# Gated cross-attention with a routed expert layer on one core: the first attention batch in a new order on four engines and the DMA queue, the first slot's rows in two halves, and a third one-hot ahead of the last selection

## What is computed

```
def _layernorm(x): m = mean(x); v = var(x); return (x - m) / sqrt(v + 1e-5)

# x: (2, 512, 1024), ctx: (2, 1024, 1024)
q1 = clip(round(layernorm(x) / s1 + z1), 0, 255);  a = (q1 - z1) * s1
q2 = clip(round(ctx / s2 + z2), 0, 255);           c = (q2 - z2) * s2
x  = x + tanh(g_xattn) * matmul(a, c)

y = layernorm(x)
logits = y @ W_gate + b_gate                       # 8 experts
top 2 experts per row
x = x + tanh(g_ffn) * mean over the 2 of relu(y @ W_e[e] + b_e[e])
```

## Time and profile before

| | |
|---|---|
| median of 3 runs | 359.78 us (358.92 to 360.76) |
| the profiled execution | 359.12 us, its span 357.4 us |
| mean granted TensorE clock | 0.964 |
| PE busy | 323.5 us, 91% of the span, 1695 instructions |
| PE weight loads busy | 251.0 us, 70% |
| DVE busy | 226.3 us, 63% |
| ACT busy | 139.9 us, 39% |
| POOL busy | 113.0 us, 32% |
| HBM | 62.43 MB read, 18.87 MB written |

### The profile page before, as it was taken

The page is one execution under the profiler, slowest core; times in us unless marked ns, Lnnn a source line. Parts: engine busy times, 40 slices in busy tenths (PEclk is TensorE's granted clock), DMA queues, the critical chain, the costliest instruction groups (busy, mean ns, idle before and its releaser), DMA issues.

```text
span 357.4 us, 6929 instructions
## 1 busy us (share of the span) xinstructions
PE 323.5 (91%) x1695; PEld 251.0 (70%) x1704; DVE 226.3 (63%) x345; ACT 139.9 (39%) x124; POOL 113.0 (32%) x135
## 2 busy tenths in 40 slices
PE   0598899999599999999999999999999999999960
PEld 0134366589547888888888888888888888888840
DVE  2898999977889653799668326832349334934220
ACT  3774878789103701656172017201154015401100
POOL 3553464000024023415335335123332333233310
PEclk9999999998579999999999999999999999999995
DMA  6999568475327986799989955975439953455233
GB/s 224 413 409 385 220 253 347 166 261 230 159 85 300 410 285 135 192 383 318 417 251 326 358 125 131 395 237 117 88 103 358 330 109 86 100 116 118 29 88 59
DMA packets 23004, 81.46 MB, mean 228 GB/s; under 512 B 3152, under 2 KB 3152, under 8 KB 22992
## 3 DMA queue, kind: packets, MB, share of 16 engines
q1 hardware_dynamic: 16656, 58.76, 42.9%
q0 software_dynamic: 6192, 22.55, 26.6%
q10 hardware_dynamic: 144, 0.01, 0.0%
HBM read 62.43 MB, written 18.87 MB: 228 GB/s over the span
## 4 chain that ended last, share of the span: by engine, by line
PE 80%; DVE 12%; issue 2%; DMA 2%; POOL 1%; ACT 0%; POOLq 0%; DVEq 0%; ACTq 0%
PE ps L1262 61%; PE ps_y L1238 5%; PE ps L1065 4%; DVE st L744 4%; PE ps_q L1124 2%; PE ps_s L1124 2%; PE ps L1042 2%; PE ps_y L1097 2%; DMA par<-in_small_dram 2%; DVE xt L808 1%; PE ps L1150 1%; PE ps L1072 1%; DVE u8c L790 1%; DVE lnv L760 1%; DVE mv L746 1%
## 5 line engine op out<-in xcount | busy, mean ns | idle before, releaser
L1262 PE MATMUL ps<-w_hi,yT_hi 128*128 x320 | 126.5, 395 | 0.5 <-DVE yT_lo L994 0.5
L1262 PE MATMUL ps<-w_hi,yT_lo 128*128 x320 | 124.8, 390 | 0.0
L1262 PE MATMUL ps<-w_lo,yT_hi 128*128 x320 | 124.5, 389 | 0.0
L880 DVE TENSOR_TENSOR w_lo<-stage,w_hi 128x2048 f32 (+1 forms) x32 | 72.0, 2287 | 13.2 <-ACT w_hi L679 11.8
L679 ACT ACTIVATE w_hi<-stage 128x2048 f32 x28 | 52.5, 1912 | 59.1 <-PE ps L1262 47.2
L504 POOL DMA_INDIRECT out_dram<-res,sidx x20 | 32.5, 1627 | 133.7 <-DVE res L1028 121.1
L1025 DVE TENSOR_TENSOR res<-ps,bias 128x512 f32<-128x512 f32 x40 | 27.6, 689 | 65.5 <-issue 34.1
L1262 PEld LDWEIGHTS ps<-w_hi,yT_hi 128*128 128x128 f32 x320 | 60.1, 188 | 12.7 <-issue 0.9
L1262 PEld LDWEIGHTS ps<-w_hi,yT_lo 128*128 128x128 f32 x320 | 60.1, 188 | 12.8
L1262 PEld LDWEIGHTS ps<-w_lo,yT_hi 128*128 128x128 f32 x320 | 60.2, 188 | 11.8
L666 ACT ACTIVATE yT_hi<-ps_y 128x1024 fp32r<-128x1024 f32 x21 | 21.4, 1020 | 114.5 <-PE ps_y L1238 114.5
(11 more groups left out here) (163 smaller groups left out, 264.7 us busy)
## 6 DMA issues: line engine op xcount, KB each, us to landing
stage<-in_L_ffn_W_e_dram SPq DMA_DIRECT2D x32, 1024.0 KB, 7.3
stage<-in_ctx_dram SPq DMA_DIRECT2D x16, 512.0 KB, 11.6
xt<-in_x_dram SPq DMA_DIRECT2D x8, 512.0 KB, 11.4
y_scratch<-y SPq DMA_DIRECT2D x8, 512.0 KB, 3.9
out_dram<-xt SPq DMA_DIRECT2D x8, 512.0 KB, 3.0
bias<-in_L_ffn_b_e_dram SPq DMA_DIRECT2D x8, 512.0 KB, 4.2
y_rows<-y_scratch,gidx POOLq DMA_INDIRECT x22
out_dram<-res,sidx POOLq DMA_INDIRECT x20, 6.4
```

The costliest lines, as they stand in the source:

```text
L880: dve.tensor_tensor(w_lo[:, dst], stage[:, CK * c:CK * (c + 1), :].rearrange("p k h -> p (k h)"), w_hi[:, dst].bitcast(f32), ALU.subtract) ...
L1262: last = pe.matmul(ps[q][:, h * 512:(h + 1) * 512], lhs[q][:, k, :], w[:, bass.ds(woff + k * D + h * 512, 512)], start=(k == 0 and lhs is ...
```

## The change

- **x and ctx loads (SP).** x tile 3 is loaded after ctx tile 7, the second batch's ctx tiles come ahead of x tiles 6 and 7, and all four chunks of the first expert's weights are issued before the first stores.
- **ACT.** `quantise_ctx(0)` is put ahead of the first `std`, tiles 1 and 2 follow it, and the order is new down to `keep_yT(2)`.
- **POOL.** It centres ctx tile 4 in place of 7 (DVE does the reverse) and x tiles 4, 5 and 7, which DVE did.
- **DVE.** `split_d` and ctx tiles 6 and 7 come before the statistics of x tile 3; the statistics of x tiles 4 to 7 come later.
- **PE.** `transpose_q1(2)` goes behind the first two folds; the column sums of the second batch are made in one piece, and the transposes of y move between the halves of `attend`.
- **One-hots (DVE).** Three, not two, before the selection of the last three tiles.
- **First slot.** Its eight transposes signal after four; ACT and DVE evacuate the two halves of four; the second weight chunk's low part is made in two pieces, one ahead of the halves and one behind; PE starts its products after the first half. `keep_clock(10)` becomes `keep_clock(6)`.

The diff's core:

```
-        POOL_CEN = (0, 1, 2, 3, 5, 7, 8, 9, 10, 11, 12, 13, 14, 15)
-        DVE_CEN = (4, 6)
+        POOL_CEN = (0, 1, 2, 3, 4, 5, 8, 9, 10, 11, 12, 13, 14, 15)
+        DVE_CEN = (6, 7)
-        POOL_Q1, DVE_Q1 = (0, 1, 2, 6), (3, 4, 5, 7)
+        POOL_Q1, DVE_Q1 = (0, 1, 2, 4, 5, 6, 7), (3,)
...
@@ POOL
             centre_ctx(0)
             centre_ctx(1)
+            centre_ctx(2)
             centre_q1(0)
-            centre_ctx(2)
             centre_q1(1)
...
@@ ACT
             std(1, 2, 2, 2)
             split_hi0(0)
+            keep_q1T(6)
+            normalise(2)
             keep_yT(2)
-            keep_q1T(6)
...
@@ DVE
             derive()
+            split_d()
+            quantise_ctx(6)
+            quantise_ctx(7)
+            centre_ctx(6)
+            centre_ctx(7)
             x_stats(3)
             scales(0, 2, 2, 2)
+            keep_colsum_lo(0)
             quantise_x(3)
             centre_q1(3)
-            centre_ctx(4)
-            quantise_ctx(6)
-            centre_ctx(6)
-            quantise_ctx(7)
-            split_d()
+            x_new(0)
...
             make_onehot(1)
+            make_onehot(2)
             select(1)
...
-            split_lo(1, 2, slice(CW, 2 * CW))
+            split_lo_row(CK)
             dve.wait_ge(s_eh, 1)
-            evacuate_lo(0)
+            evacuate_lo(0, slice(0, KT // 2)).then_inc(s_el, 1)
+            dve.wait_ge(s_eh, 2)
+            evacuate_lo(0, slice(KT // 2, KT)).then_inc(s_el, 1)
+            split_lo_row(CK + 1).then_inc(s_lo, 1)
...
@@ PE
             fold(0)
             fold(1)
+            transpose_q1(2)
             transpose_q1(3)
...
-            transpose_y(0)
-            column_sums(KT + 4, KT + 6)
+            column_sums(KT + 4, 2 * KT)
             pe.wait_ge(s_rs, 1)
             transpose_q1(5)
-            transpose_y(1)
-            column_sums(KT + 6, 2 * KT)
             attend_after(4)
             attend_half(4, 0)
-            gate(0)
+            transpose_y(0)
             attend_half(4, 1)
             fold(4)
-            transpose_y(2)
+            transpose_y(1)
+            gate(0)
             attend_after(5)
             attend_half(5, 0)
             gate(1)
             transpose_q1(6)
             attend_half(5, 1)
             fold(5)
-            transpose_y(3)
+            transpose_y(2)
             attend_after(6)
             attend_half(6, 0)
+            transpose_y(3)
...
-            transpose_slot(0)
-            keep_clock(10)
+            for k in range(KT):
+                last = pe.transpose(ps_y[:, k, :], y_rows[0][:, k * P:(k + 1) * P], ident_f[:, :])
+                if k == KT // 2 - 1:
+                    last.then_inc(s_t0, 1)
+            last.then_inc(s_tp, 1)
+            keep_clock(6)
```

More of the change, by code:

```diff
@@ L322, in _ @@
                 load_x(i)
-            for k in (0, 1):
+            for k in (0, 1, 2):
                 load_ctx(k)
             load_x(2)
-            load_ctx(2)
-            load_x(3)
             for k in range(3, KT):
                 load_ctx(k)
-            for j in range(TPB):
-                load_x(TPB + j)
-                load_ctx(KT + j)
+            load_x(3)
+            load_ctx(KT)
+            load_ctx(KT + 1)
+            load_x(4)
+            load_ctx(KT + 2)
+            load_x(5)
+            load_ctx(KT + 3)
+            load_ctx(KT + 4)
             sp.dma_start(wg[:, :, :], W_gate.rearrange("(k p) e -> p k e", p=P)).then_inc(s_wg, 16)
-            for k in range(KT + TPB, 2 * KT):
+            for k in range(KT + 5, 2 * KT):
                 load_ctx(k)
-            load_w0(0)
-            load_w0(1)
+            load_x(6)
+            load_x(7)
+            for c in range(NCH):
+                load_w0(c)
             store_y(0)
             store_y(1)
-            load_w0(2)
-            load_w0(3)
             store_x_new(0)
@@ L441, in _ @@
             centre_ctx(1)
+            centre_ctx(2)
             centre_q1(0)
-            centre_ctx(2)
             centre_q1(1)
             centre_ctx(3)
+            centre_ctx(4)
             centre_ctx(5)
-            centre_ctx(7)
             centre_ctx(8)
+            centre_ctx(9)
+            centre_ctx(10)
             centre_q1(2)
-            for k in range(KT + 1, 2 * KT):
+            for k in range(KT + 3, 2 * KT):
                 centre_ctx(k)
+            centre_q1(4)
+            centre_q1(5)
             pool.wait_ge(s_att, TPB)
@@ L596, in _ @@
             act.activation(lnv[:, 0, T1, 0:1], eps[:, :], ACT.Sqrt)
+            act.wait_ge(s_inv, 1)
+            quantise_ctx(0)
             std(0, 0, 2, 1)
-            quantise_ctx(0)
             quantise_ctx(1)
+            quantise_ctx(2)
             quantise_x(0)
-            quantise_ctx(2)
             quantise_x(1)
-            std(0, 2, 2, 2)
[L604 to L608, removed]
+            quantise_ctx(3)
+            quantise_ctx(4)
+            keep_q1T(0)
+            quantise_ctx(5)
+            keep_q1T(1)
+            quantise_ctx(8)
+            keep_colsum_hi(0)
+            std(0, 2, 2, 2)
+            quantise_ctx(9)
+            quantise_ctx(10)
             quantise_x(2)
-            quantise_ctx(8)
+            quantise_ctx(11)
             keep_q1T(2)
[L612 to L617, removed]
             keep_q1T(3)
             quantise_ctx(12)
-            quantise_x(5)
[L621 to L626, removed]
+            quantise_ctx(13)
+            quantise_ctx(14)
+            std(0, 4, 2, 3)
+            quantise_ctx(15)
+            quantise_x(4)
+            quantise_x(5)
             keep_q1T(4)
             keep_q1T(5)
-            std(1, 2, 2, 2)
+            std(1, 0, 2, 1)
+            keep_colsum_hi(1)
+            normalise(1)
+            keep_yT(0)
+            sum_q1(4)
+            std(0, 6, 2, 4)
             keep_yT(1)
[L631 to L634, removed]
             quantise_x(6)
             quantise_x(7)
+            std(1, 2, 2, 2)
             split_hi0(0)
+            keep_q1T(6)
+            normalise(2)
             keep_yT(2)
-            keep_q1T(6)
             std(1, 4, 1, 3)
@@ L685, in step @@
                 act.wait_ge(s_tp, slot + 2)
-                evacuate_hi(slot + 1, 1 - q)
+                evacuate_hi(1 - q, slice(0, KT)).then_inc(s_eh, 2)
                 with act.If(nxt > 0):
@@ L948, in _ @@
             slot_matrix(1)
-            for i in range(2, NT):
+            for i in range(3, NT):
                 make_onehot(i)
@@ L1252, in step @@
                 pe.wait_ge(s_free, slot * HB + 1)
-                pe.wait_ge(s_el, slot + 1)
+                pe.wait_ge(s_el, slot * 2 + 1)
                 for h in range(HB):
@@ L1256, in step @@
                         if h == 0 and k == CK:
+                            pe.wait_ge(s_el, slot * 2 + 2)
                             pe.wait_ge(s_g[1 - q], turn * 16 + (16 if q == 0 else 32))
```

59 lines of the change are left out of this document (30 added, 29 removed).

## The result

| | before | changed |
|---|---|---|
| median, same chip | 359.57 us (358.92 to 360.76, 4 runs) | 364.21 us (364.08 to 365.30, 4 runs) |
| profiled execution | 359.12 us, span 357.4 | 365.30 us, span 363.6 |
| mean granted TensorE clock | 0.964 | 0.954 |

The account below looks back on a forecast made before the run. PE was taken to bound the kernel, mostly waiting for DVE, with hardly a gap from 43.60 to 71.33. Terms -0.9 + 4.05 - 0.4 - 0.45 = +2.3 on the median of 359.78 gave 362.1 us; 8-in-10 range 358.7 to 364.3.

Parts of the forecast that it names:

- step 3: Second batch: three new PE waits, for y of tile 0, q1 of tile 6 and y of tile 2; +4.05 us.
- the second wait: Second batch: PE waits for q1 of x tile 6 from POOL, 9.8 against 9.25 of PE work; 0.56 us.
- step 1: First scales on DVE: held by POOL's centring of ctx tiles 0 to 2, ready at 14.05 instead of 12.66.
- the fifth is held: First scales: DVE's fifth instruction waits for POOL's centring of tile 1; if not, scales are ready at 13.05.
- step 2: First batch, up to the sums of q1 at 43.60: a gain, -0.9 us, bounds -2.4 to 0.
- bound of 0 for the latest rise: First batch: no gain if PE's clock rises only at 24.3 and all of POOL's holds on DVE apply.
- the forecast rise at 22.7: First batch: PE's clock goes from 1.2 to 2.4 GHz at 22.7, 5.1 after its last gap.
- between the two bounds: First batch: as the number of slow matmuls varies by run, anything from -2.4 to 0 us may come.
- Steps 4 to 6: Moved loads cost 0; third one-hot gives -0.4 us; first slot in halves gives -0.45 us.
- The faster one: Rival, chance 0.14: clock falls behind the last gates, saving 2.2; with early front and low bounds -2.4 us, 357.4.
- Much slower: Rival, chance 0.18: no first-batch gain, a longer second batch, one-hot and slot gains kept; +4.1 us, 363.9.
- the late rise and the fourth hold: Clock rises late, so the first batch gains 0; one more hold adds 0.9 us to the second batch's waits.

Follow-up runs that it names:

- The three runs with products added in front: Changed kernel plus twelve dummy products (363.63); new first batch, mended with nine, under old second batch (365.82); changed kernel plus both ACT moves and twenty (360.25).
- the square root first: Changed kernel with one ACT call moved: std(1, 0) goes ahead of keep_q1T(5); 364.14 us, ratio 1.0111 to the kernel before.
- the slot alone: Kernel before with only the first slot's part of the change (halves, weight chunk in two pieces, keep_clock(6)); 360.05 us, ratio 0.9987.
- more added work: Changed kernel with two ACT calls moved (std(1, 0) earlier, split_hi0(0) later) and twenty dummy PE products; 360.25 us, ratio 0.9983 to the kernel before.
- the two runs with added products: Kernel before with the first slot in halves, third one-hot, and 6 or 12 dummy products around the last gates; 359.02 and 359.01 us.
- one or both ACT edits: Changed kernel with std(1, 0) ahead of keep_q1T(5) (364.14), split_hi0(0) behind normalise(2) (363.53), or both moves (365.18 us).
- the trace shown above: Kernel before with the first slot in two halves and the third one-hot, none of the first batch's changes; 360.19 us, ratio 0.997.

## Why the prediction was off by half

- **Right: the sign of the whole, and the second batch.** All three waits of step 3 are there, with the engines named: 1.46 (forecast 1.6), 0.43 (0.56), 1.76 (1.85), 3.65 against 4.0; the stretch grew by 3.4 against 4.05. (The terms listed for the second wait add up to 9.9, not 9.8, which would make it 0.7.)
- **Right: step 1.** Timeline of DVE in the changed kernel:

```profile
10.88 0.65 DVE L772 SCALAR_TENSOR_TENSOR lnv<-mv,eps,lnv 128x2 f32<-128x2 f32 x1
...
11.96 0.90 DVE L776 TENSOR_SCALAR lnv<-lnv,drv 128x2 f32<-128x2 f32 x1
...
13.10 0.94 DVE L778 TENSOR_SCALAR lnv<-lnv,par 128x2 f32<-128x2 f32 x1
```

  and of POOL:

```profile
10.49 1.05 POOL L428 TENSOR_SCALAR q<-u8c 128x1024 bf16<-128x1024 uint8 x1 [6.58 <-ACT u8c L534]
11.80 2.22 POOL L428 TENSOR_SCALAR q<-u8c 128x1024 bf16<-128x1024 uint8 x2 [0.26 <-ACT u8c L534]
```

  The second, fifth and seventh instruction end with POOL's three centrings, and the scales end at 14.04 (forecast 14.05). The choice that the fifth is held was right. The Trainium skill (SBUF — State Buffer, Who interferes with whom) gave the same answer, and the trace agrees.
- **Wrong: step 2, -0.9 forecast, +2.3 measured.** The walk held to the correction (fold at 31.16, forecast 31). Then two terms failed. DVE's quantising and centring of x tile 3 were priced at 0.8 and some 0.6, with one hold of 1.06; both were held by POOL's centrings at 31.12 and 32.25:

```profile
31.05 1.67 DVE L788 TENSOR_SCALAR u8x<-xt,lnv 128x1024 uint8<-128x1024 f32 x1
32.75 1.41 DVE L796 TENSOR_SCALAR q<-u8x 128x1024 bf16<-128x1024 uint8 x1
```

  so that the two took 3.1, not 2.5, and with 0.3 from ahead of them (DVE's half ended at 31.02, not 30.7) PE attended tile 2 at 35.53, not 34.5: 1.0. And the forecast took each product there at 0.23, when the gaps it had itself put ahead of them (for the correction, for q1 of tile 3, for the slab) took the clock down: 5.84 - 3.63 = 2.2. The three runs with products added in front, where these ran at full speed, show that this was the gaps' doing. The forecast used the clock only for when it rises, never for whether it falls again. Its bound of 0 for the latest rise lay 2.3 below what came, and below all four other traces of the same front (+0.8 to +1.4).
- **The Trainium skill's rule on the clock.** The prediction quoted the Trainium skill (TensorE: Matmul & The Clock Gate, Part 1): activity releases the throttle, and the number of slow matmuls isn't to be fitted. The traces agree with the second: the first eight products of the attention, in eight traces with the same instructions up to there, take

```profile
19.68 3.51 PE L1084 MATMUL ps<-q,q1T 128*128 128x512 bf16 x8
```

```profile
19.62 2.16 PE L1084 MATMUL ps<-q,q1T 128*128 128x512 bf16 x8
```

  in the changed kernel and with the square root first, and between these two in the others. (The slow pace is read from the products; the granted clock of the profile reads 1.00 here.) So the forecast rise at 22.7, which came at about 23.0 in the profiled execution, was luck: it was taken from the one rise in the kernel before. And "between the two bounds" was wrong, since the range had no second fall in it.
- **Steps 4 to 6.** The moved loads cost nothing on PE's path. Gates and one-hots gave -0.3 for -0.4: five one-hots take 3.07, as costed, while the gates are 0.4 slower. At the last weight chunk PE was 8.39 behind the transposes (forecast 8.25; before 8.81, which the forecast read as 8.7), and at the slot's end -0.3 is left, for -0.45. The first product came 3.28 behind them, not 2.2, though DVE's first half was there after some 2.0 (its two halves take 1.29 from 112.15 on); what PE waited for isn't settled (with the square root first, the slot alone and more added work it came after 2.53 to 2.75), and the weight chunk behind it makes it worth nothing.
- **Rivals.** The faster one needed the clock to fall behind the last gates. It fell in front of them, as before; the two runs with added products show that 2.4 of gate time lay there, as its 2.2 had it. "Much slower" (363.9) is nearest to the 364.2 measured, yet by another mechanism than the late rise and the fourth hold it was made of. The range ended at 364.3 because of that rival, so that it held 364.2 is luck too.
- **What failed, in one line.** Step 2: the front was forecast to win 0.9 and lost 2.3 in the profiled execution (0.8 to 1.4 in four others). The term at fault is the clock, put at "rises once" (2.2 in this trace), and beside it the holds of DVE's two instructions and a start that was late by 0.3 (1.0 together).

## What to carry to other kernels

When a change opens a gap on PE, price it as a range, from the gap alone to the gap plus the work behind it at the lower clock, and look at the granted clock of that stretch before you believe a sum of waits. When a repair takes a wait away and the time stays, look for the next wait and for slow products behind it, and at more than one trace where the clock is at play. A few products of no use in a gap that can't be closed were cheap here (twenty of them, with two moves on ACT, took 4 us back). And an order written by hand hangs together over its stages: the new front under the old middle was 1.4% slower than the kernel before, and no faster than the changed one.

## What the runs showed of the chip

Behind gaps of about 1 us the granted clock fell to 0.50, that is to 1.2 GHz, for some 2 to 6 us, and not always for as long: behind gaps of 1.07, 1.37 and 0.28 the sixteen products took 5.84; in the kernels with one or both ACT edits, whose gaps are 1.06 or 2.16, 1.37, and 0.28 or 0.70, they took 4.62, 5.31 and 5.31. A wait of 0.43 ahead of x tile 6 left the clock alone in two traces and had slow products behind it in a third (1.89 against 3.55). A wait of 1.76 ahead of the fp32 transposes at 69.00 left the clock alone, and so did the one of 1.02 ahead of x tile 3 before. Nor does a busy PE keep it: it fell in the gates of 8 columns at 86 with PE busy without a gap, as in all twelve traces without added products there, and at 74.53 in the trace shown above; with six or twelve products of 512 columns among the last gates it stayed up until they were all but done (two traces). What separates the gaps that cost the clock from those that don't stays open.
